# Selective scan on one core: two-step projections, remainders on TensorE, and two of twelve increments on GpSimd

## The chip, the cores and the metric

One core of a Trainium2 chip runs the whole program. The metric is device time in microseconds from start to end of one execution, lower is better. The engines are PE (TensorE: matmul, with PEld its weight load), DVE (VectorE), ACT (ScalarE), POOL (GpSimd) and SP (SyncE), which here issues all DMAs of the part that changes. A name with a q (SPq, PEq) is an engine's sequencer.

## The reference, cut to what matters

The program is a convolution-like state-space block, then an attention and an expert block; only the first is touched. `x` is 4 images of 192 channels and 32 x 32 positions, so L = 1024. After a group norm:

```python
# 4 directions k: row order, column order, and both reversed
xs    = stack([x0, x1, reversed(x0), reversed(x1)])
x_dbl = einsum('bkdl,kcd->bkcl', xs, x_proj_weight)       # 6 + 16 + 16 rows
dts, Bs, Cs = split(x_dbl)                                # 6, 16, 16
dt = softplus(einsum('bkrl,kdr->bkdl', dts, dt_projs_weight) + bias)
def step(h, ...):                  # 16 states for each of 192 channels
    h = h * exp(dt * A) + (dt * u) * B
    return h, sum over n of h * C
y = merge of the 4 directions of (scan(step) + Ds * u)
```

The states are 4 images x 4 directions x 192 channels x 16 = 49,152 recurrences of 1024 steps each.

## The kernel before, in words

`prepare` norms x into `s.X` (96 partitions, two halves of channels, 1024 positions) and readies the weights. `scan` then runs `Fori` over the 4 images with 8 **units** written out inside, 32 units in all. A unit is one direction (p: row or column order; r: forward or backward) and one half f of the channels, so 96 channels with 16 states each. It is cut into 12 **tiles** t of 8 channels x 16 states = 128 partitions x 1024 positions. A tile's scan runs in two halves (24 half tiles q, two for each t), as PSUM holds 512 columns to a bank. `n` counts units, `g` half tiles.

For each tile:

- SP loads `decay[:, t % 4, :]` with a broadcasting DMA (L632, `load`): 8 rows of dt, each repeated on 16 partitions, 128 x 4 KB = 512 KB. It is issued when tile t - 4 has been scanned (DR = 4 buffers).
- ACT makes exp(dt * A) of it in place (L501).
- PE spreads dt*u from `stack` over the 128 partitions (L425, a bf16 matmul with three bf16 parts stacked on 96 rows, so that nothing is lost) into a ring of 4 PSUM banks `psU`.
- DVE multiplies that by B (L558, `product`, one half tile ahead) and scans (L614); the second half starts from the last state of the first and waits for its end.
- POOL multiplies the states by C (L528), in place in `hs` (HR = 6 buffers).
- PE sums the 16 states of each channel, three tiles at a time (L387, `sum_states`, four trips a unit), into `psY`; DVE takes `psY` into `s.Y` after every second unit (L567 in row order, with the skip term D*u; L571 in column order, which reads and writes with a stride).

Between the tiles the next units' inputs are made. The projection of dt (L352 `project`, weights `w_dt` that `prepare` has multiplied out to 96 x 96 blocks) runs at half tiles 16 to 19 for the unit two ahead; ACT does softplus at t = 9 to 11 (L454 to L460), POOL adds its two terms at t = 9 (L538) and multiplies by u at t = 11 (L544), giving `dt` and `dtu`. SP stores `dt` to DRAM (`store`), from which the loads read. `dtu` is split into three bf16 parts by ACT (L468, L471) and POOL (L531, L534) at t = 2 to 6 of the next unit, and SP copies the parts to `stack` with 9 DMAs of 64 KB at t = 4, 5 and 7. B and C for a unit are projected by PE straight into their spread form of 128 rows and copied by ACT to `bc` (L480). ACT makes a turned copy `xt` of x for the column order (L510).

All engines run their instructions in the order written, and so does SP. The waits that set the order around a tile are these, in PE's and DVE's parts:

```python
pe.wait_ge(scan_done, g + (S0 - UR + 1))      # half tile q - 4 scanned: its bank is free
if q % 6 == 0: v.wait_ge(summed, ...)         # the hs buffer is free
v.wait_ge(decay_ready, n * TILES + (t + 1))   # exp made
```

## Time and profile before

| | us |
|---|---|
| time, median of 3 runs (lowest, highest) | 3095.22 (3094.96, 3102.87) |
| profiled execution, its own time | 3110.97 |
| its span | 3108.9 |
| first product of the scan to the last scan's start | 75.5 to 1540.3 |
| one unit of the scan, mean of 32 | 45.8 |
| mean granted clock of TensorE, as a share of 2.4 GHz | 0.834 |

The profile comes from the one profiled execution. "Busy" is the time in which an engine works on instructions; the idle time in brackets stands before an instruction, with what ended it. The granted clock is that which TensorE got: 1.00 stands for 2.4 GHz and 0.50 for 1.2 GHz. The DMA share is the mean busy share of the core's 16 DMA engines.

### The profile page before, as it was taken

Reading aid. Unit: us, or ns where it says so; the run is one execution under the profiler, and the core shown is the slowest. Engines: PE = TensorE matmul, PEld = TensorE weight load, DVE = VectorE, ACT = ScalarE, POOL = GpSimd, SP = SyncE. Lnnn points to the kernel's source line nnn. Section 1 sums busy time; section 2 is a strip of 40 time slices with the busy share of each in tenths; the row PEclk is TensorE's granted clock in tenths of the full one; section 3 lists DMA queues with packets and bytes.
Section 4 is the critical chain, followed back from the end, with each engine's and each line's share of the span. In section 5 each row is a group of like instructions: output and inputs, shape, how many; then the busy total and the mean of one; then the engine's idle time right before and its main releaser. Section 6 shows DMA issues by size and latency. Waiting matters only on the chain. (4 is left out here: it accounts for less than half of the span.)

```text
span 3108.9 us, 33979 instructions
## 1 busy us (share of the span) xinstructions
PE 2521.1 (81%) x9156; PEld 920.0 (30%) x9156; DVE 2223.0 (72%) x3030; ACT 1424.7 (46%) x1949; POOL 1311.6 (42%) x677
## 2 busy tenths in 40 slices
PE   4677677776677766776668689999999889999999
PEld 2111111111111111111124123232232246666766
DVE  4999999999999998999755688787878631111112
ACT  3444544445444444444456147676767522222221
POOL 1788878787788877788751100000000200000000
PEclk9777767777677777777758689999999889999999
DMA  3555555555555555555512603131313400000000
GB/s 88 144 167 165 160 152 166 154 155 159 157 168 162 166 146 152 160 152 163 152 47 80 104 2 43 23 42 24 42 23 42 87 1 6 5 5 5 5 5 10
DMA packets 101755, 286.76 MB, mean 92 GB/s; under 512 B 14878, under 2 KB 19137, under 8 KB 101569
## 3 DMA queue, kind: packets, MB, share of 16 engines
q1 hardware_dynamic: 100506, 284.94, 35.1%
q8 instruction: 52, 0.85, 0.1%
q14 instruction: 95, 0.78, 0.1%
q10 hardware_dynamic: 1102, 0.19, 0.0%
HBM read 239.66 MB, written 25.88 MB: 85 GB/s over the span
## 5 line engine op out<-in xcount | busy, mean ns | idle before, releaser
L528 POOL TENSOR_TENSOR hs<-hs,bc 128x1024 f32<-128x1024 f32 x384 | 900.4, 2355 | 224.9 <-DVE hs L614 224.2
L501 ACT ACTIVATE decay<-decay,a_neg 128x1024 f32<-128x1024 f32 x384 | 440.4, 1148 | 666.2 <-DMA decay<-dt_rows 652.3
L425 PE MATMUL psU<-stack,spread_sel 96*128 96x512 bf16 x768 | 361.1, 487 | 425.0 <-DVE hs L614 346.3
L1446 DVE TENSOR_REDUCE mx<-ps 128x1 f32<-128x512 f32 x864 | 539.3, 682 | 117.7 <-PE ps L1285 112.4
L558 DVE TENSOR_TENSOR psU<-psU,bc 128x512 f32<-128x512 f32 x768 | 514.4, 673 | 25.9 <-issue 13.4
L1421 ACT ACTIVATE P<-ps 128x512 f32<-128x512 f32 x768 | 417.6, 599 | 249.3 <-PE ps L1297 225.2
L614 DVE TENSOR_TENSOR_SCAN hs<-decay,psU 128x512 f32<-128x512 f32 x384 | 464.7, 1210 | 72.6 <-PE psY L387 52.4
L614 DVE TENSOR_TENSOR_SCAN hs<-decay,hs,psU 128x512 f32<-128x512 f32 x384 | 487.5, 1269 | 1.1
L387 PE MATMUL psY<-hs,state_sel 128*32 128x512 f32 x1572 | 401.5, 855 | 23.2 <-DVE Y L571 11.2
L1719 DVE SCALAR_TENSOR_TENSOR acc<-psE,gate,acc 128x192 f32<-128x192 f32 x128 | 53.4, 417 | 448.5 <-PE psE L1619 445.5
L1285 PE MATMUL ps<-ks,qs 96*128 96x512 bf16 x864 | 345.0, 404 | 34.8 <-DMA ks<-qk_parts 24.2
L425 PEld LDWEIGHTS psU<-stack,spread_sel 96*128 96x128 bf16 x768 | 71.1, 100 | 992.2 <-DVE hs L614 818.4
L1610 PE MATMUL psH<-Zf,w 96*128 x768 | 334.3, 592 | 1.1 <-DVE pr L1677 1.1
L1657 ACT ACTIVATE hid<-psH,b 128x512 f32<-128x512 f32 x192 | 131.5, 687 | 382.5 <-PE psH L1610 382.5
L1297 PE MATMUL ps<-qs,ks 99*128 99x512 bf16 x768 | 294.4, 383 | 0.0
L1619 PEld LDWEIGHTS psE<-w,hid 128*128 128x128 f32 x1536 | 251.2, 190 | 13.4 <-issue 13.4
L1619 PE MATMUL psE<-w,hid 128*128 128x192 f32 x1536 | 254.2, 326 | 0.0
L1310 PE MATMUL psO<-P,v_now 128*32 128x512 f32 x1536 | 206.2, 609 | 0.0
L1610 PEld LDWEIGHTS psH<-Zf,w 96*128 96x128 f32 x768 | 144.7, 190 | 171.8 <-issue 170.8
L1285 PEld LDWEIGHTS ps<-ks,qs 96*128 96x128 bf16 x864 | 83.8, 98 | 314.7 <-DVE mx L1446 233.1
L1225 POOL COPY v_now<-V 128x1024 f32 (+1 forms) x15 | 15.5, 1038 | 320.1 <-PE psO L1310 320.0
L1217 POOL TENSOR_TENSOR nm<-zero,top 128x32 f32<-128x32 f32 x13 | 3.3, 253 | 344.5 <-DVE top L1450 344.5
(237 smaller groups left out, 2280.3 us busy)
## 6 DMA issues: line engine op xcount, KB each, us to landing
decay<-dt_rows SPq DMA_DIRECT2D x388, 512.0 KB
stack<-parts SPq DMA_DIRECT2D x297, 64.0 KB, 5.5
dt_rows<-dt SPq DMA_DIRECT2D x33, 384.0 KB, 7.1
qs<-qk_parts SPq DMA_DIRECT2D x90, 128.0 KB, 6.7
ks<-qk_parts SPq DMA_DIRECT2D x90, 128.0 KB, 7.2
qk_parts<-qparts SPq DMA_DIRECT2D x16, 576.0 KB, 3.7
w<-in_L_ffn_w_dram SPq DMA_DIRECT2D x8, 576.0 KB, 9.9
X<-in_x_dram SPq DMA_DIRECT2D x4, 768.0 KB, 9.7
```

What stands on the lines that cost most here:

```text
L387: m = pe.matmul(psY[BLK * j:BLK * j + BLK, c, :], s.state_sel[:, trip, :], hs[:, (3 * trip + j) % HR, CH * c:CH * c + CH], start=(trip == ...
L425: pe.matmul(psU[:, q % UR, :], s.spread_sel[:, gg, :], stack[:, ui % 2, j, CH * pos:CH * pos + CH], start=True, stop=True).then_inc(dtu_sp ...
L501: nc.scalar.activation(decay[:, t % DR, :], decay[:, t % DR, :], ACT.Exp, scale=s.a_neg[:, col:col + 1]).then_inc(decay_ready, 1)
L528: pool.tensor_tensor(h, h, bc[:, 2 * p + r, 1, :], ALU.mult).then_inc(hc_ready, 1)
L558: v.tensor_tensor(u, u, bc[:, 2 * p + r, 0, CH * pos:CH * pos + CH], ALU.mult).then_inc(dbu_ready, 1)
L614: v.tensor_tensor_scan(h, da, du, init, ALU.mult, ALU.add).then_inc(scan_done, 1)
L1285: m = pe.matmul(ps1[:, bank, :], qs[0:KQ, hg, head, 128 * qt:128 * qt + 128], ks[0:KQ, hg, head, CH * c:CH * c + CH], start=True, stop=not ...
L1297: m = pe.matmul(ps2[:, bank, :], ks[0:KM, hg, head, 128 * kt:128 * kt + 128], qs[0:KM, hg, head, CH * qc:CH * qc + CH], start=True, stop=n ...
L1421: nc.scalar.activation(P[:, kt % 2, head, :], ps2[:, bank, :], ACT.Exp).then_inc(exp_done, 1)
L1446: v.reduce_max(mx[:, slot, u:u + 1], ps1[:, (slot * MAXES + u) % R, :], AX.X).then_inc(max_done, 1)
L1610: m = pe.matmul(psH[:, t % 3, :], w1[:, e, f, 128 * t:128 * t + 128], s.Z[:, b, f, CH * c:CH * c + CH], start=(f == 0), stop=(f == 1))
L1619: m = pe.matmul(psE[:, tt % 2, 0:D], hid[:, e % 2, t, 128 * tt:128 * tt + 128], w2[:, e, t, :], start=(t == 0), stop=(t == HT - 1))
```

## The change: what it does

Prepared weights: `w_dt` is no longer multiplied out. A projection now runs in two steps: `inputs` (two matmuls with `w_xd`, 128 rows that hold the 6 + 32 rows of both r of one p) gives `xd` once for each image and p, and `steps` makes the 96 rows of a unit from 6 rows of it. B and C of `xd` go to DRAM (`keep_xd`) and come back spread over 128 partitions by DMA (`load_bc`, two DMAs of 512 KB for each of the four directions of an image, at t = 2 and 4 of units 5, 6, 7 and 0).

The order of units becomes f, p, r, so all four directions add up in `psY` and ACT takes it after four units (`take`); PE adds the skip term itself (`skip`, with a diagonal). There is no `xt`: PE and POOL read and write in column order with a stride (`turned`, and `h.rearrange` in `sum_states`).

The second and third bf16 part of dt*u come from TensorE (`remainder`: identity times `dtu` minus the parts known, in `psP`, which ACT casts), so POOL's two subtractions go.

For tiles 5 and 11 (POOL_TILES) there is no spread by PE and no product by DVE. SP loads the 8 rows of dt*u from DRAM (`keep_dtu`, `load_rep`, 512 KB each), POOL multiplies them by B, and ACT writes its exp for these tiles into `psU`.

The making of dt and dt*u moves forward: softplus from t = 9 to 11 to t = 5 to 7, the sum and the product on POOL from t = 9, 11 to t = 4, 5, the first cast from t = 4 of the next unit to t = 11. `hs` gets 8 buffers and `decay` 6.

The diff, cut to its core:

```diff
-        HR, DR, UR = 6, 4, 4
+        HR, DR, UR = 8, 6, 4
+        POOL_TILES = (5, 11)
 # TensorE
+                def inputs(out, nb, p, c):
+                    for h in range(2):
+                        m = pe.matmul(out, s.w_xd[:, p, h, :], turned(s.X[:, nb, h, :], p)[:, 16 * c:16 * c + 16, :],
+                                      start=(h == 0), stop=(h == 1))
+                    m.then_inc(xd_proj, 1)
+                def remainder(c, known, ready):
+                    cs = slice(CH * c, CH * c + CH)
+                    m = pe.matmul(psP[0:HC, c, :], s.ident[0:HC, 0:HC], dtu[:, cs], start=True, stop=False)
+                    for i in range(known):
+                        m = pe.matmul(psP[0:HC, c, :], s.minus_bf[:], parts[:, i, cs], start=False, stop=(i == known - 1))
+                    m.then_inc(ready, 1)
...
-                                pe.wait_ge(scan_done, g + (S0 - UR + 1))
-                                pe.matmul(psU[:, q % UR, :], s.spread_sel[:, gg, :],
-                                          stack[:, ui % 2, j, CH * pos:CH * pos + CH],
-                                          start=True, stop=True).then_inc(dtu_spread, 1)
-                                z_side(q, *unit_ahead(b, ui), n + 2)
-                                bc_side(q, b, ui, n)
+                                if t not in POOL_TILES:
+                                    pe.wait_ge(scan_done, g + (S0 - UR + 1))
+                                    pe.matmul(psU[:, q % UR, :], s.spread_sel[:, gg, :],
+                                              stack[:, ui % 2, j, CH * pos:CH * pos + CH],
+                                              start=True, stop=True).then_inc(dtu_spread, 1)
+                                if t == 1:
+                                    pe.wait_ge(mid_ready, n * 2 + (c + 3))
+                                    remainder(c, 2, tail_ready)
+                                if t == 3:
+                                    if c == 0:
+                                        pe.wait_ge(xd_ready, nb * 4 + (2 * order(nu)[1] + 2))
+                                    pe.wait_ge(lo_ready, n * 2 + (c + 3))
+                                    steps(nu, c)
+                                if t == 6 and ui in XD_UNITS:
+                                    pe.wait_ge(z_taken, n * 2 + 6)
+                                    inputs(psP[:, c, :], (b + 1) % NB, XD_UNITS[ui], c)
+                                if t == 10:
+                                    if c == 0:
...
+                                        pe.wait_ge(dtu_ready, n + 3)
+                                        pe.wait_ge(hi_ready, n + 3)
+                                    remainder(c, 1, rest_ready)
 # ScalarE
+                            to = at = decay[:, t % DR, :]
+                            if t in POOL_TILES:
+                                to = psU[:, 2 * t % UR:2 * t % UR + 2, :]
...
+                                act.wait_ge(scan_done, n * (2 * TILES) + (2 * t - 2 + S0))
...
+                            if t == 11:
+                                act.wait_ge(stacked[(ui + 1) % 2], in_stack(b, ui + 1))
+                                act.wait_ge(dtu_ready, n + 3)
+                                nc.scalar.copy(parts[:, 0, :], dtu[:]).then_inc(hi_ready, 1)
 # GpSimd
+                            if t + 3 in POOL_TILES:
+                                i = POOL_TILES.index(t + 3)
+                                pool.wait_ge(rep_landed[i], n * 16 + 16)
+                                pool.tensor_tensor(rep[:, i, :], rep[:, i, :], bc[:, slot, 0, :], ALU.mult).then_inc(rep_ready, 1)
 # SyncE
+                def load_dt(slot, t):
+                    d = rows_of(t)
+                    src = s.dt_dram[slot, d:d + DD, :].unsqueeze(1).broadcast_to([DD, N, L])
+                    sp.dma_start(decay[:, t % DR, :], src).then_inc(landed[t % DR], 16)
+                def load_rep(slot, i):
+                    src = s.dtu_dram[slot, i].unsqueeze(1).broadcast_to([DD, N, L])
+                    sp.dma_start(rep[:, i, :], src).then_inc(rep_landed[i], 16)
+                def load_bc(slot, which=(0, 1)):
+                    p, r = slot // 2, slot % 2
+                    for i in which:
+                        at = BLK * r + N * i
+                        src = s.bc_dram[p, at:at + N, :].unsqueeze(0).broadcast_to([DD, N, L])
+                        sp.dma_start(bc[:, slot, i, :], src).then_inc(bc_landed[slot], 16)
...
+                load_bc(0)
+                sp.wait_ge(dt_ready, 1)
+                keep_dt(0)
...
+                for t in range(DR):
+                    load_dt(0, t)
+                sp.wait_ge(dtu_stored, 32)
+                for i in range(2):
+                    load_rep(0, i)
+                for part, (ready, n) in enumerate(((hi_ready, 1), (mid_ready, 2), (lo_ready, 2))):
+                    sp.wait_ge(ready, n)
+                    stack_up(part, 0)
+                load_bc(1)
+                load_bc(2)
...
+                            if t == 2 and ui in (5, 6, 7, 0):
+                                sp.wait_ge(hc_ready, n * TILES + (TILES + START))
+                                load_bc((ui - 5) % UNITS, (0,))
+                            if t == 4 and ui in (5, 6, 7, 0):
+                                load_bc((ui - 5) % UNITS, (1,))
...
+                            if t in POOL_TILES:
...
+                                load_rep((ui + 1) % 4, i)
```

At the end of `scan` SP waits for every load that was issued, those for a unit that doesn't come among them, as it did before.

## Rows read from the trace of the kernel before

**Rows 1.** The page: busy time of each engine, and DMA share in tenths

```profile
PE 2521.1 (81%) x9156; PEld 920.0 (30%) x9156; DVE 2223.0 (72%) x3030; ACT 1424.7 (46%) x1949; POOL 1311.6 (42%) x677
...
DMA  3555555555555555555512603131313400000000
```

**Rows 2.** Busy time by window: the scan, from first product to last scan

```profile
core 0: us, PE busy (x) PEld busy (x) DVE busy (x) ACT busy (x) POOL busy (x), PEclk, DMA share, GB/s
75.50:1541.00 1465.50, 1034.24 (x2827) 228.33 (x2827) 1373.96 (x1552) 684.45 (x709) 1171.21 (x509) 0.73 0.54 158
```

**Rows 3.** Who waited for whom in 130 to 1500 us: total, times, longest

```profile
ACT decay L501 <- DMA decay<-dt_rows: 609.0, 299, 5.1
...
DVE hs L614 <- PE psY L387: 49.3, 43, 2.0
...
DVE hs L614 <- ACT decay L501: 18.2, 24, 1.6
```

**Rows 4.** DMA issues in 130 to 1500 us

```profile
decay<-dt_rows SPq DMA_DIRECT2D x360, 512.0 KB
```

**Rows 5.** Two windows of 2 us in the scan (columns as in rows 2)

```profile
514.00:516.00 2.00, 2.00 (x4) 0.53 (x2) 2.00 (x3) 0.00 (x0) 1.79 (x2) 0.50 0.51 125
...
540.00:542.00 2.00, 1.80 (x9) 0.25 (x7) 2.00 (x3) 0.67 (x2) 2.00 (x2) 1.00 0.51 203
```

**Rows 6.** Two units that follow each other (columns as in rows 2)

```profile
683.30:736.10 52.80, 32.78 (x92) 7.68 (x95) 45.49 (x52) 22.32 (x24) 39.14 (x18) 0.69 0.55 153
736.10:778.70 42.60, 30.03 (x87) 6.44 (x81) 40.24 (x46) 24.16 (x24) 34.00 (x16) 0.74 0.53 158
```

**Rows 7.** DVE in order of time: start, length, instruction

```profile
501.50 1.21 DVE L614 TENSOR_TENSOR_SCAN hs<-decay,psU 128x512 f32<-128x512 f32 x1
502.63 0.68 DVE L558 TENSOR_TENSOR psU<-psU,bc 128x512 f32<-128x512 f32 x1
503.21 1.27 DVE L614 TENSOR_TENSOR_SCAN hs<-decay,hs,psU 128x512 f32<-128x512 f32 x1
...
504.98 1.21 DVE L614 TENSOR_TENSOR_SCAN hs<-decay,psU 128x512 f32<-128x512 f32 x1
```

**Rows 8.** Groups by line and shape, 0 to 1850 us

```profile
L528 POOL TENSOR_TENSOR hs<-hs,bc 128x1024 f32<-128x1024 f32 x384 | 900.4, 2355 | 224.9 <-DVE hs L614 224.2
...
L501 ACT ACTIVATE decay<-decay,a_neg 128x1024 f32<-128x1024 f32 x384 | 440.4, 1148 | 666.2 <-DMA decay<-dt_rows 652.3 <-issue 13.3
...
L531 POOL TENSOR_TENSOR rest<-dtu,parts 96x1024 f32<-96x1024 f32 x32 | 68.0, 2125 | 14.4 <-ACT parts L468 14.3
...
L468 ACT CAST parts<-dtu 96x1024 bf16<-96x1024 f32 x33 | 34.0, 1030 | 2.5 <-DVE dtu L580 2.5
...
L571 DVE TENSOR_TENSOR Y<-Y,psY 96x1024 f32 x8 | 16.0, 2006 | 0.0
...
L567 DVE SCALAR_TENSOR_TENSOR Y<-X,d_sum,psY 96x1024 f32 x8 | 10.0, 1251 | 0.0
```

**Rows 9.** PE in order of time, at 1.2 GHz (first two) and 2.4 GHz

```profile
503.31 1.93 PE L387 MATMUL psY<-hs,state_sel 128*32 128x512 f32 x6
...
578.52 1.91 PE L352 MATMUL psP<-xt,w_c 96*128 96x512 f32 x2
...
585.80 1.02 PE L352 MATMUL psP<-xt,w_c 96*128 96x512 f32 x2
```

**Rows 10.** All engines in order of time: start of the scan

```profile
21.94 5.43 PE L206 MATMUL ps_prep<-wdt,wx 6*96 6x192 f32 x16 [1.10 <-DVE wdt L233]
...
51.09 2.67 SPq L632 DMA_DIRECT2D decay<-dt_rows  x4
...
74.88 0.61 PE L425 MATMUL psU<-stack,spread_sel 96*128 96x512 bf16 x1 [11.71 <-DMA stack<-parts]
```

**Rows 11.** All engines in order of time: after the scan

```profile
1549.94 1.91 DVE L571 TENSOR_TENSOR Y<-Y,psY 96x1024 f32<-96x1024 f32 x1 [8.37 <-PE psY L387]
...
1552.14 2.09 SPq L801 DMA_DIRECT2D raw<-in_x_dram  x4
```

More of the change, by code:

```diff
@@ L266, in _ @@
                 own.wait()
+                v.wait_ge(gp, 3)
+                for f in range(2):
+                    own(v.tensor_scalar(s.d_diag[:, f, :], s.ident[0:HC, 0:HC], s.d_sum[:, f:f + 1], None, ALU.mult))
+                own(v.tensor_scalar(s.minus_bf[:], s.ident[0:HC, 0:HC], -1.0, None, ALU.mult))
+                own.wait()
+        nc.clear_and_free_semaphores(sems)
+        nc.all_engine_barrier()
 def scan(nc, w, s):
@@ L380, in sum_states, with steps @@
-                def sum_states(n, pair, r, trip, c, first=None):
+                def inputs(out, nb, p, c):
[3 more added lines that the diff above has]
+                    m.then_inc(xd_proj, 1)
+                def steps(nu, c):
+                    f, p, r, k = order(nu)
+                    pe.matmul(psP[0:HC, c, :], s.w_dt[BLK * r:BLK * r + R, p, HC * f:HC * f + HC],
+                              xd[BLK * r:BLK * r + R, p, CH * c:CH * c + CH], start=True, stop=True).then_inc(z_proj, 1)
@@ new lines, in remainder, with skip @@
+                def remainder(c, known, ready):
[4 more added lines that the diff above has]
+                    m.then_inc(ready, 1)
+                def skip(b, f, c):
+                    pe.matmul(psY[0:HC, c, :], s.d_diag[:, f, :], s.X[:, b, f, CH * c:CH * c + CH], start=True, stop=False)
@@ L382, in sum_states @@
+                def sum_states(n, ui, trip, c):
+                    p = order(ui)[1]
                     if c == 0:
-                        if trip == 0 and r == 0:
-                            pe.wait_ge(y_taken, pair + (1 + START))
                         pe.wait_ge(hc_ready, n * TILES + (TILES + 3 * trip + 3 + START))
                     for j in range(NBLK):
+                        h = hs[:, (ui * TILES + 3 * trip + j) % HR, :]
+                        h = h.rearrange("p (w h) -> p h w", h=HH) if p else h.rearrange("p (h w) -> p h w", h=HH)
@@ new lines, in z_end, with part @@
+                def z_end(n1):
+                    act.wait_ge(z_taken, n1 * 2 + 2)
+                    nc.scalar.activation(soft[:], soft[:], ACT.Exp, scale=-1.0).then_inc(exp_own, 1)
+                    act.wait_ge(exp_own, n1 + 1)
+                    nc.scalar.activation(soft[:], soft[:], ACT.Ln, bias=s.one[0:HC, :]).then_inc(log_ready, 1)
+                def part(i, n1, c, rest, ready):
+                    act.wait_ge(rest, n1 * 2 + (c + 1))
+                    nc.scalar.copy(parts[:, i, CH * c:CH * c + CH], psP[0:HC, c, :]).then_inc(ready, 1)
@@ new lines, in take @@
+                def take(b, f, last):
+                    act.wait_ge(summed, last + SUM0)
+                    nc.scalar.copy(s.Y[:, b, f, :], psY[0:HC, :, :].rearrange("p c l -> p (c l)")).then_inc(y_taken, 1)
+                nc.scalar.preload_act_table_set("natural_log_exp_and_others")
+                for p in range(2):
+                    for c in range(2):
+                        act.wait_ge(xd_proj, 2 * p + c + 1)
+                        nc.scalar.copy(xd[:, p, CH * c:CH * c + CH], (psU if p else psP)[:, c, :]).then_inc(xd_ready, 1)
@@ new lines, in _ @@
+                for c in range(2):
+                    z_half(0, 0, c)
+                z_end(0)
+                act.wait_ge(dtu_ready, 1)
+                nc.scalar.copy(parts[:, 0, :], dtu[:]).then_inc(hi_ready, 1)
+                for c in range(2):
+                    part(1, 0, c, rest_ready, mid_ready)
+                for c in range(2):
+                    part(2, 0, c, tail_ready, lo_ready)
+                act.wait_ge(dt_stored, 16)
+                for c in range(2):
+                    z_half(1, 1, c)
@@ L494, in _ @@
+                z_end(1)
+                act.wait_ge(stacked[0], STACK_INC)
+                act.wait_ge(dtu_ready, 2)
+                nc.scalar.copy(parts[:, 0, :], dtu[:]).then_inc(hi_ready, 1)
                 with act.Fori(0, NB, 1) as b:
@@ L506, in _ @@
[L506 to L512 removed]
+                            if t == 1:
+                                for c in range(2):
+                                    part(1, n + 1, c, rest_ready, mid_ready)
@@ new lines, in _ @@
+                            if t == 3:
+                                for c in range(2):
+                                    part(2, n + 1, c, tail_ready, lo_ready)
+                            if t == 4 and ui % 4 == 0:
+                                take(b if ui else (b + (NB - 1)) % NB, 1 - f, n * SUB)
+                            if t == 5:
+                                act.wait_ge(dtu_ready, n + 2)
+                                act.wait_ge(dt_stored, n * 16 + 32)
+                                z_half(nu, n + 2, 0)
```

420 lines of the change are left out of this document (193 added, 227 removed).

## The prediction

> **What bounds the kernel now.** I read the page first [rows 1]: DVE looks like the engine to relieve, and the DMA engines look half idle, at five tenths in every slice of the scan. The window over the scan alone [rows 2] puts numbers on both: DVE busy 1374 of 1465.5 us (94%), POOL 80%, PE 71% at a granted clock of 0.73, DMA share 0.54. A unit is 1465.5 / 32 = 45.8 us.
>
> Then DVE in order of time [rows 7]. From 501.50 to 504.98 is one tile with no gap: scan 1.13, product 0.58, scan 1.19, product 0.58 (start to start), 3.48 us. Twelve tiles are 41.8 us, and the takes (8 of 1.25 and 8 of 2.01 us in 32 units [rows 8]) add 0.8. With some 0.2 at the end of a unit that makes 42.8, so DVE stands still for 3.0 us of a unit. The waits [rows 3] say for whom: sums of PE (49 us in 30 units) and exps of ACT (18). Neither is a busy engine. ACT itself waits 609 us, and for one thing: the decay loads.
>
> The DMA share is the row that the reader is to look at twice. A share of 0.50 that never falls can be 16 engines half idle or 8 of them never idle. Two windows decide it [rows 5]: both show 0.51, while one moves 125 GB/s and the other 203. If the engines had slack, the share would go up and down with the bytes. It stays at one half while the speed changes by 1.6, so eight engines are always busy, and what varies is how long a packet takes. Two neighbouring units show what that does [rows 6]: the same work takes 52.8 us at 153 GB/s and 42.6 us at 158, with the share 0.55 and 0.53; DVE works 45.5 and 40.2 us of them (the windows cut tiles, so these differ a little), that is 86% and 94%. The short unit is DVE's own 42.8, the long one is not.
>
> So two things stand within a few per cent of each other: DVE (42.8 us a unit) and the eight DMA engines that carry the decay loads. Their account, from rows 2: of the 0.54, 0.50 are these eight, always on. The other 0.04 x 16 engines over 8 engines is 8% of 45.8 = 3.7 us a unit in which the upper eight work too; that is the stack copies and the store of dt, which use all 16 and so cost the lower eight the same 3.7. There remain 42.1 us for 12 loads [rows 4]: **3.51 us a load** of 512 KB as a mean. The windows give its bounds, 524 KB at 203 GB/s = 2.6 us and at 125 = 4.2.
>
> **The change, part by part.**
>
> *DVE.* Each of the two POOL tiles loses two products of 0.58; one of the scans now has to wait for the full end of the one before (1.21 after its start, not 1.13, plus the signal), which gives 0.1 back. 2 x 1.05 = 2.1 us a unit. The takes go to ACT: 0.8. DVE comes to 42.8 - 2.9 = 39.9 us.
>
> *POOL.* Minus two subtractions of 2.1 [rows 8], plus two products of 2.35 less overlap: 12 + 2 + 2 operations of 2.31 = 37.0 us, as before. With a stride, which no POOL row here has, dt*u costs between 2.35 and 1.6 times that (DVE with and without: 2.01 and 1.25 [rows 8]); I take 1.6 in half the units, mean 37.7. It hides under 39.9.
>
> *PE.* A float32 matmul of 512 columns is a pair of 1.91 us at the low clock and 1.02 at the high one [rows 9]. Out go 8 pairs of projections and 4 bf16 spreads; in come 4 pairs and 6 bf16 (remainders), 2 pairs (steps), 1 (inputs), 0.5 (skip). That is equal within a pair. Reading `hs` with a stride in half the units is unknown: from nothing to 1.6 times, which would lift 4 trips x 2 x 1.93 = 15.4 us by 9 at worst. PE now: 1034/32 = 32.3; then up to 37 as a mean. Hidden; I take nothing.
>
> *ACT* is at 21 us a unit and stays there: two casts of 1.03 become one and four halves, one take in four units is added.
>
> *A new wait.* PE's remainder at t = 10 stands between the spreads of half tiles 20 and 21 and waits for `hi_ready` n + 3. ACT makes it after the exp of tile 11, which may not write `psU` until tile 9 is scanned. So from the end of tile 9: exp 1.05, cast 1.03, remainder 0.5 + 0.2 to 1.0 + 0.4 behind a signal each (0.1), spread 0.4 to 0.6: product 21 comes 3.7 to 4.9 us later, and DVE has nothing else, as scan 20 stands behind product 21. I take 4.0: DVE's unit is **43.9**, and the shortening that DVE was to get is nearly gone. ACT's exp of tile 5 has the same wait for tile 3, but DVE has 3.0 us of tile 4 to do in that time and the exp takes 1.15, so it is free.
>
> *SP and the DMAs.* Nothing is taken from the queue: still 12 decay loads (also for tiles 5 and 11), 9 copies, one store. Added for each unit: 2 loads of dt*u (512 KB each), one of B or C (8 for 8 units), two small stores of 8 rows (one packet an engine, 3.51/16 = 0.22 us each) and a quarter of an `xd` store. The dt*u load has the form of the decay load. The B and C load repeats 16 rows 8 times, its outer size is 8 too, but no row of before shows it: at best it uses 16 engines (half of 3.51), at worst it is a decay load. I take a decay load, the nearest row.
>
> The unit's DMA time is then 15 x 3.51 + 3.7 + 0.5 = **56.9 us** on the same eight engines, against 43.9 for DVE, 38 for POOL and 37 for PE. Its bounds are 15 x 2.6 + 4.2 = 43.2 and 15 x 4.2 + 4.2 = 67. Deeper buffers (6, 8) do not help: they cover lateness, not a lack of throughput.
>
> On that load the Trainium skill (DMA: Bandwidth & Descriptors, section on why a DMA increments its semaphore by 16) says that a DMA is spread over the largest number up to 16 that divides the outermost sizes of both sides, always the lowest-numbered ones. By it every load here gets 8, as the share of 0.50 in rows 5 agrees with, and B and C too; were those on 16, the unit would be 55.1.
>
> *Start and end.* Before, PE's 5.4 us of multiplied-out weights delayed the norm (DVE waited 5.9) [rows 10]; that goes, the scan begins some 4 us earlier. But before the first spread the queue must now move 2 B/C, 6 decay and 2 dt*u loads, and then the 9 copies, not 4 and 9. The queue starts at about 44 rather than 51; 44 + 10 x 3.51 + 3.7 + 3 for the store's round trip = 86 against 74.9 [rows 10]. From there 4 + 32 x 15 = 484 loads and 32 x 4.2 are to be moved, and SP waits for all: 86 + 1699 + 134 = 1919. Before, the same count, 74.9 + 384 x 3.51 + 32 x 3.7 = 1541, is the scan's end [rows 2], and the block ended at 1552 [rows 11] with the last sums, under which its last loads lay; now the loads end last. 1919 - 1552 = 367 us more. What follows the scan is the same.
>
> **The sum.** The profiled execution spans 3108.9 and took 3110.97; the same with the change would be 3476. It lies 15.8 us (0.5%) over the median of the runs, 3095.2, so the median goes to 3095 + 367 = 3462, I say **3460 us**, 12% slower.
>
> **Rivals.**
>
> *A, the one forecast (0.69):* bound by eight DMA engines at 3.0 to 3.8 us a load, 3210 to 3600 by the same count. For it: the constant 0.51 and the unit of 52.8 us that the same work took when packets were slow.
>
> *B, the same bound with faster packets (0.11):* 2.8 to 3.0 us. The copies come in one bunch a unit instead of three, so the stream is disturbed less often. At 3.0 us the count is 80 + 484 x 3.0 + 134 = 1666, 114 more, 3209; at 2.8 it is 78 + 1355 + 134 = 1567, 3110.
>
> *C, faster (0.13):* the loads take 2.6 us throughout, as in the second window of rows 5, because the long packets of before come from something that the change removes. Then 43.2 us of DMA lie under 43.9 of DVE and its new wait: 32 x (43.9 - 45.8) = -61, start +2 to +5, so about 3040. It decides from 2.7 us a load downward, where the count falls under 1552. Against it: within the trace of before 3.51 is the mean of 388 loads, and at the very start, with no other engine at work, the queue was no faster: four loads and nine copies from 51.1 to 74.9 [rows 10]. The skill's page on DMA gives a limit of some 358 GB/s for a core's HBM traffic (section Specifications); the new unit moves 8.9 MB, which by that would take 25 us and bound nothing; no window of the scan comes near it.
>
> *D, slower still (0.04):* column order. If PE reads a stride of 32 floats at a fourth of its speed, the sums of those units cost 15.4 x 3 = 46 us more, PE comes to 78 us in half the units, the mean is (78 + 57)/2 = 67.5, and the time 3095 + 367 + 32 x 10.6 = 3800. The skill (SBUF — State Buffer, the note on cachelines in its section on ports) speaks for some price of such strides. DVE's 2.01 against 1.25 [rows 8] says 1.6, with which D does not happen.
>
> *E, no change (0.03):* a load of 2.7 to 2.8 us, where the count gives the 1552 of before.
>
> **How the numbers follow.** The forecast is A's time at the mean of before. The range holds A and B whole, 3110 (2.8 us a load) to 3600 (3.8 us): 0.69 + 0.11 = 0.80; C, D and E lie outside. It is that wide because one number, the time of a load, carries all of it, and the trace has it anywhere between 2.6 and 4.2 us. About 0.3% (9 us) is what a measurement of this kernel cannot tell from no change. Faster is C, 0.13; the same is E, 0.03; slower is A, B and D, 0.84.
>
> **What would show it.** Right: in the scan the DMA share stays at 0.55 or so with DVE's busy share down to 70%; GB/s hardly above 160 as a mean; ACT waits for decay, dt*u or both, and now DVE waits for ACT's exp in most tiles; units of some 57 us; the scan's DMAs outlast its last scan. Wrong: a share below 0.5 in parts of each unit, or GB/s near 200 all through, units of 44 us, and a gap of 4 us on DVE before half tile 21. The prediction fails most easily on 3.51 us, which I measured but cannot derive.

## The result, and the profile after

| | before | after |
|---|---|---|
| time, median (lowest, highest; runs) | 3099.05 (3094.96, 3114.12; 4) | 3321.32 (3314.73, 3326.98; 4) |
| ratio to before, 95% interval | | 1.0707 [1.0662, 1.0752] |
| span of the profiled execution | 3108.9 | 3325.1 |
| mean granted clock of TensorE | 0.834 | 0.828 |

The medians here and below are of all runs; the ratios leave out a run that took over 1.5% longer than the fastest of its kernel. The change makes the kernel 222 us slower. The prediction said 3460 us with a range of 3110 to 3600: slower, as forecast, by about 60% of the size.

The page of the kernel after: busy time, the DMA share in tenths, and GB/s in the same 40 slices. The rows of before are [rows 1].

```profile
PE 2608.1 (78%) x9176; PEld 912.0 (27%) x9176; DVE 2125.1 (64%) x2885; ACT 1418.1 (43%) x1994; POOL 1342.0 (40%) x675
...
DMA  4555555555555555555553170322223130000000
GB/s 100 161 162 169 157 177 194 160 178 175 154 194 189 166 160 172 196 167 171 187 165 113 58 115 2 40 27 35 35 27 40 21 81 5 5 5 5 5 5 10
```

DVE has lost 98 us of work while the span has grown by 216, so the time went into waiting. The DMA row still reads five tenths throughout, but the bytes a second went up: 173 GB/s in the scan against 158 [rows 2]. The window over the scan, from first product to last scan:

```profile
core 0: us, PE busy (x) PEld busy (x) DVE busy (x) ACT busy (x) POOL busy (x), PEclk, DMA share, GB/s
109.10:1761.40 1652.30, 1127.26 (x2857) 227.03 (x2859) 1282.96 (x1408) 676.03 (x754) 1206.63 (x511) 0.73 0.53 173
```

A unit is now 51.6 us (1652.3 / 32) against 45.8. DVE works 40.1 us of it against 42.9 and stands still for 11.5 against 2.9. The 216 us of the span by stretch:

| stretch | before | after | change |
|---|---|---|---|
| start to first product | 75.5 | 109.1 | +33.6 |
| first product to last scan's start | 1464.8 | 1652.3 | +187.5 |
| last scan's start to the next part's first load | 11.8 | 12.7 | +0.9 |
| everything behind | 1556.8 | 1551.0 | -5.8 |

The next view is of the waits in 130 to 1500 us (total, times, longest), and it names what DVE waits for. Compare [rows 3]: there ACT's wait for the loads was 609 us, here it is 291 and, for the exps that go to `psU`, 33.

```profile
ACT psU L528 <- DVE hs L645: 342.6, 44, 12.2
DVE psU L602 <- PE psU L431: 298.7, 92, 8.6
ACT decay L528 <- DMA decay<-dt_rows: 290.9, 153, 7.1
...
PE psP L369 <- ACT parts L553: 164.4, 27, 10.0
...
DVE hs L645 <- ACT decay L528: 5.3, 6, 2.2
```

DVE waits 299 us for PE's spread and 5 us for ACT's exp. If the loads set the pace, most of the wait would be for exps, since that is how a load of dt reaches DVE. (There is a second way, which these rows hide; it comes below.) Where in the unit DVE waits is found by adding up the idle times in DVE's order of time by half tile, over 32 units: before product 21 it is 196 us (6.1 a unit, in all 32 of them, never under 5.0), before 13 or 14 it is 70 us, nearly all of it in units 4 and 6 of each image (counted from 0), and before 8 it is 54. Before the first product of a unit it is only 14, in the first unit of the last three images (4.5 to 4.7 each); the remaining 35 us are scattered. One of the 32 places before product 21, by DVE, ACT and PE in order of time:

```profile
1031.63 1.27 DVE L645 TENSOR_TENSOR_SCAN hs<-decay,hs,psU 128x512 f32<-128x512 f32 x1
1038.05 0.70 DVE L602 TENSOR_TENSOR psU<-psU,bc 128x512 f32<-128x512 f32 x1 [5.15 <-PE psU L431]
...
1032.94 1.12 ACT L528 ACTIVATE psU<-decay,a_neg 128x1024 f32<-128x1024 f32 x1 [3.58 <-DVE hs L645]
1033.99 1.03 ACT L553 CAST parts<-dtu 96x1024 bf16<-96x1024 f32 x1
...
1029.82 0.57 PE L431 MATMUL psU<-stack,spread_sel 96*128 96x512 bf16 x1
1035.16 1.99 PE L369 MATMUL psP<-dtu,ident 96*96 96x512 f32 x2 [4.77 <-ACT parts L553]
1036.95 0.63 PE L371 MATMUL psP<-parts,minus_bf 96*96 96x512 bf16 x1
1037.38 0.63 PE L431 MATMUL psU<-stack,spread_sel 96*128 96x512 bf16 x1
```

The reader is to follow the chain from top to bottom: the second scan of tile 9 ends at 1032.90; ACT's exp of tile 11, which had waited for it, ends at 1034.06; the cast ends at 1035.02; PE's remainder pair and its bf16 part end at 1037.6; the spread at 1038.0; and only then DVE has a product to make. These are 5.15 us, in which DVE has nothing. PE had no work for 4.77 us before its remainder, which then ran at 1.2 GHz: 1.99 us is the low clock's time [rows 9].

In 21 of the 32 places the gap is that of these rows, or within 0.3 us of it. In the other 11 it is 6.3 to 8.7 us, because the exp of tile 11 waited longer, not for the scan but for its own load. This is the second way from the loads to DVE: by the exp, the cast, the remainder and the spread, so it stands in the row of DVE's waits for PE. What goes beyond the usual 5.15 us comes to 31 us in all. One of the 11:

```profile
411.27 1.12 ACT L528 ACTIVATE psU<-decay,a_neg 128x1024 f32<-128x1024 f32 x1 [4.01 <-DMA decay<-dt_rows]
...
416.39 0.70 DVE L602 TENSOR_TENSOR psU<-psU,bc 128x512 f32<-128x512 f32 x1 [8.65 <-PE psU L431]
```

### The profile page after: what moved, and what is told of

The parts are those of the page before. It is cut to its first block and busy times, and to the rows that moved or that the text cites. A ratio compares the mean times of both kernels' runs of the same rounds, so it can differ in the third digit from the quotient of the medians.

```text
span 3325.1 us, 34486 instructions
## 1 busy us (share of the span) xinstructions
PE 2608.1 (78%) x9176; PEld 912.0 (27%) x9176; DVE 2125.1 (64%) x2885; ACT 1418.1 (43%) x1994; POOL 1342.0 (40%) x675
## 5 line engine op out<-in xcount | busy, mean ns | idle before, releaser
L602 DVE TENSOR_TENSOR psU<-psU,bc 128x512 f32<-128x512 f32 x640 | 431.3, 678 | 394.1 <-PE psU L431 393.6
L385 PE MATMUL psY<-hs,state_sel 128*32 128x512 f32 x1560 | 502.5, 1054 | 41.4 <-POOL hs L571 35.9
L528 ACT ACTIVATE decay<-decay,a_neg 128x1024 f32<-128x1024 f32 x320 | 364.7, 1149 | 330.0 <-DMA decay<-dt_rows 329.5
L431 PE MATMUL psU<-stack,spread_sel 96*128 96x512 bf16 x640 | 284.0, 470 | 256.7 <-DVE hs L645 256.2
L645 DVE TENSOR_TENSOR_SCAN hs<-decay,hs,psU 128x512 f32<-128x512 f32 x320 | 406.8, 1271 | 2.3
L645 DVE TENSOR_TENSOR_SCAN hs<-decay,psU 128x512 f32<-128x512 f32 x320 | 386.6, 1208 | 8.0 <-ACT decay L528 8.0
L369 PE MATMUL psP<-dtu,ident 96*96 96x512 f32 x268 | 200.5, 841 | 242.2 <-ACT parts L553 196.6
L431 PEld LDWEIGHTS psU<-stack,spread_sel 96*128 96x128 bf16 x640 | 60.1, 102 | 828.7 <-DVE hs L645 597.2
L528 ACT ACTIVATE psU<-decay,a_neg 128x1024 f32<-128x1024 f32 x64 | 71.5, 1118 | 454.4 <-DVE hs L645 413.8
```

Source lines behind the costliest of these rows:

```text
L385: m = pe.matmul(psY[BLK * j:BLK * j + BLK, c, :], s.state_sel[:, trip, :], h[:, 16 * c:16 * c + 16, :], start=False, stop=(trip == SUB - 1 ...
L431: pe.matmul(psU[:, q % UR, :], s.spread_sel[:, gg, :], stack[:, ui % 2, j, CH * pos:CH * pos + CH], start=True, stop=True).then_inc(dtu_sp ...
L528: nc.scalar.activation(to, at, ACT.Exp, scale=s.a_neg[:, col:col + 1]).then_inc(decay_ready, 1)
L602: v.tensor_tensor(u, u, bc[:, 2 * p + r, 0, CH * pos:CH * pos + CH], ALU.mult).then_inc(dbu_ready, 1)
L645: v.tensor_tensor_scan(h, da, du, init, ALU.mult, ALU.add).then_inc(scan_done, 1)
```

## The experiments

The ratio is always to the kernel before on the same chip, in the same job. "Scan" runs in this table, and in the windows of the experiments, from the start of the first scan (3 to 6 us behind the first product) to the start of the last, and a unit is a 32nd of it. By this measure a unit is 45.6 us before the change and 51.5 after it.

| kernel | median us | ratio, 95% interval | scan, us | share, GB/s |
|---|---|---|---|---|
| before | 3099.05 | | 79.8 to 1540.3 | 0.54, 159 |
| after | 3321.32 | 1.0707 [1.0662, 1.0752] | 112.2 to 1761.4 | 0.53, 174 |
| before_plus3 | 3163.08 | 1.0195 [1.0121, 1.0269] | 78.4 to 1601.2 | 0.55, 185 |
| before_plus6 | 3316.34 | 1.0613 [1.0529, 1.0697] | 78.1 to 1744.5 | 0.54, 199 |
| before16 | 3077.43 | 0.9909 [0.9882, 0.9936] | 73.8 to 1513.9 | 0.65, 170 |
| after16 | 3294.67 | 1.0618 [1.0559, 1.0677] | 98.0 to 1730.2 | 0.79, 185 |
| after_late | 3203.89 | 1.034 [1.026, 1.0419] | 107.5 to 1635.1 | 0.55, 188 |
| after16_late | 3196.93 | 1.0279 [1.0244, 1.0314] | 92.9 to 1625.5 | 0.83, 197 |
| mix | 3213.63 | 1.0291 [1.0211, 1.0371] | 105.1 to 1660.1 | 0.55, 184 |
| mix16 | 3097.21 | 0.9976 [0.9951, 1.0002] | 91.9 to 1534.9 | 0.88, 209 |
| after_cast | 3170.59 | 1.0203 [1.0148, 1.0257] | 113.5 to 1604.9 | 0.55, 192 |
| after16_cast | 3188.3 | 1.0285 [1.0234, 1.0336] | 97.9 to 1607.5 | 0.85, 199 |
| mix16b | 3101.37 | 0.9988 [0.9965, 1.0012] | 78.4 to 1537.3 | 0.87, 208 |

In the expectations, D is the theory of the prediction (the eight DMA engines bound the changed kernel) and W its rival (the new waits in the order of the engines do).

**1. before_plus3: is the kernel before at the limit of the eight DMA engines?** Three loads of the decay load's form are added to each unit. They read 8 rows of the input into a buffer that nobody reads; the rest is unchanged.

```diff
+                            if t in (1, 5, 9):
+                                sp.wait_ge(spare_in, n * 48 + (16 * (t // 4) + 16))
+                                sp.dma_start(spare[:], w.x[0, 0:DD].rearrange("d h w -> d (h w)").unsqueeze(1)
+                                             .broadcast_to([DD, N, L])).then_inc(spare_in, 16)
```

> The kernel before with three more loads of 512 KB in each unit, in the form of the decay load (8 rows of x, repeated 16 times), into a spare buffer that nobody reads; no engine waits for them. Theory D: a unit grows by three loads, 3 x 3.15 to 3 x 3.51 = 9.5 to 10.5 us less the slack of 0.5, so 3095 + 32 x 5.8 to 10 = 3280 to 3415; 3280 is what the changed kernel's own loads of 3.15 us give. Rival W: within 15 us of 3095.

Measured: 1.0195 [1.0121, 1.0269], 3163 us. A quarter more loads lengthens the unit from 45.6 to 47.6 us, so a load more costs 0.65 us, not 3.5. Neither expectation held: 3163 lies between D's 3280 and W's 3095. The share stays at 0.55 and the GB/s rise from 158 to 185. The eight engines that looked never idle had a good part of their speed left.

**2. before_plus6: and where does it end?** The same with six extra loads a unit (at every odd t), again into a buffer that nobody reads.

> The kernel before with six more loads of 512 KB a unit (one at each odd t) into the spare buffer. Three more cost 1.8 us a unit. If a load really takes the 3.51 us that the trace of before gives, 18 loads are 67 us, time 3770. If the engines keep 2.5 to 2.9 us a load when they always have work, 18 loads and 3.7 are 49 to 56 us, time 3200 to 3420.

Measured: 1.0613 [1.0529, 1.0697], 3316 us. The next three loads cost 4.5 us a unit (52.1 against 47.6), so this kernel is near a limit for much of the time, though not for all. By the prediction's account it spends (52.1 - 3.7) / 18 = 2.7 us a load. Window and waits of before_plus6:

```profile
core 0: us, PE busy (x) PEld busy (x) DVE busy (x) ACT busy (x) POOL busy (x), PEclk, DMA share, GB/s
78.10:1744.50 1666.40, 1016.94 (x2814) 222.17 (x2812) 1383.63 (x1549) 684.70 (x709) 1168.93 (x508) 0.71 0.54 199
```

```profile
PE psU L427 <- DMA stack<-parts: 187.6, 25, 9.9
...
DVE hs L616 <- ACT decay L503: 131.9, 87, 5.2
```

```profile
SPq L661 <- DMA spare<-in_x_dram: 711.5, 157, 9.8
```

This is what a kernel looks like whose loads come late throughout: 199 GB/s, PE waits for the stack copies behind them, and DVE waits 132 us for exps. The share is 0.54, as in the kernel before that moves 158 GB/s. The share does not tell the two apart; the waits do. Part of the lateness is the experiment's own: there is one spare buffer, so SP, which issues in order, waited 711 us in 130 to 1500 us for the spare load before to land, and every decay load behind it waited too (before_plus3 has no such row). So 2.7 us is an upper value for what a load costs on these engines.

**3. before16 and after16: the same loads on sixteen engines.** `dt` (and dt*u) is stored twice in DRAM, so that the outer size of a load is 16; the bytes of a load are the same.

```diff
-                src = s.dt_dram[par, d:d + DD, :].unsqueeze(1).broadcast_to([DD, N, L])
+                src = s.dt_dram[par, d:d + DD, :, :].rearrange("d c l -> (d c) l").unsqueeze(1).broadcast_to([2 * DD, N // 2, L])
```

> The kernel before, with dt kept twice in DRAM so that a decay load has 16 source rows, each repeated 8 times, in place of 8 rows repeated 16 times: the same bytes into the same places, an outermost size of 16. Theory D (eight DMA engines bound both kernels): the loads spread over 16 engines, the DMA share varies with the bytes, DVE's stalls of 3.0 us a unit go, unit 42.8 to 43.5, time 3010 (2995 to 3035). Rival W (DMA was never a bound, what costs is the order of waits on PE, ACT and DVE): 3095, unchanged.

> The changed kernel with dt and dt*u kept twice in DRAM, so that decay and dt*u loads have 16 source rows (B and C loads as they are). Theory D: the DMA bound goes, what is left is DVE's 39.9 and its wait of 5 us at half tile 21: unit 46 (shortest unit now), time 3321 - 32 x 5.5 - 12 at the start = 3130 (3090 to 3180). Rival W (the 12.3 us that DVE stands before products are all the order of waits): within 30 us of 3321.

Measured: before16 0.9909 [0.9882, 0.9936], after16 1.0618 [1.0559, 1.0677]. The share rises to 0.65 and 0.79, so the loads do use more engines. The rule of the Trainium skill that the prediction weighed (DMA: Bandwidth & Descriptors, the section on why a DMA increments its semaphore by 16), by which the outer sizes set the count, agrees with these shares. Window and waits of after16:

```profile
98.00:1730.20 1632.20, 1114.20 (x2849) 225.12 (x2846) 1278.18 (x1407) 667.13 (x754) 1207.36 (x511) 0.74 0.79 185
```

```profile
DVE psU L602 <- PE psU L431: 289.7, 73, 10.8
...
ACT decay L528 <- DMA decay<-dt_rows: 92.8, 49, 4.0
```

ACT's wait for the loads falls from 291 to 93 us (for the exps that go to `psU`, which have a scan to wait for as well, it goes from 33 to 88), and the wait of DVE for PE hardly moves, from 299 to 290. The time falls by 27 us out of 222 (3294.67 against 3321.32), 14 of which lie ahead of the first scan (98.0 against 112.2). D, which asked for 3130, falls here: loads on sixteen engines do not set the changed kernel free. They are not quite out of it, though. The gap before product 21 is 209 us in after16, no less than the 196 of the changed kernel, and in 12 of its 32 places the exp of tile 11 still waits for its load (45 us beyond the usual 5.15). All 12 are in units 5, 7 and 0 of an image, where SP also issues loads of B and C, which this run left on 8 rows.

before16 is the fastest kernel of the study, some 28 us (0.9% of 3110) below before; here too neither expectation held (3010, or no change). Its schedule is unchanged, DVE's wait for exps (18 us before) is gone, and ACT's for loads falls from 609 to 435.

**4. after_cast: one line.** ACT makes the first cast one tile earlier, ahead of the exp of tile 11, which has to wait for tile 9. All work is done, and the loads are unchanged.

```diff
-                            if t == 11:
+                            if t == 10:
                                 act.wait_ge(stacked[(ui + 1) % 2], in_stack(b, ui + 1))
                                 act.wait_ge(dtu_ready, n + 3)
                                 nc.scalar.copy(parts[:, 0, :], dtu[:]).then_inc(hi_ready, 1)
```

> The changed kernel with one thing moved on ACT: the first cast of the next dt*u stands before the exp of tile 11 (at t = 10) and no longer behind it, so PE's remainder at t = 10 need not wait for the end of tile 9. Nothing on PE, DVE, POOL or in the loads is changed. Theory W: the 6.1 us a unit before product 21 fall to about 1 (PE's own 2.6 us of remainder stay between two spreads), worth up to 160 us. Theory D says that with 8 source rows the DMA engines (15 x 2.7 to 3.0 + 4.2 = 45 to 49) take over: 3200 to 3260, and then some of the wait comes back as waits for spreads or exps.

Measured: 1.0203 [1.0148, 1.0257], 3171 us, 151 less than after. Window, waits, and the same place of a unit in order of time:

```profile
113.50:1604.90 1491.40, 1065.01 (x2852) 218.28 (x2846) 1280.51 (x1407) 673.35 (x754) 1202.72 (x510) 0.77 0.55 192
```

```profile
DVE psU L602 <- PE psU L431: 149.2, 76, 7.6
...
PE psP L369 <- ACT parts L553: 10.7, 6, 2.7
```

```profile
1037.05 1.03 ACT L553 CAST parts<-dtu 96x1024 bf16<-96x1024 f32 x1
1038.22 1.07 PE L369 MATMUL psP<-dtu,ident 96*96 96x512 f32 x2 [1.16 <-ACT parts L553]
1039.12 0.38 PE L371 MATMUL psP<-parts,minus_bf 96*96 96x512 bf16 x1
1039.15 1.12 ACT L528 ACTIVATE psU<-decay,a_neg 128x1024 f32<-128x1024 f32 x1 [1.08 <-DVE hs L645]
1039.34 0.38 PE L431 MATMUL psU<-stack,spread_sel 96*128 96x512 bf16 x1
1039.76 0.70 DVE L602 TENSOR_TENSOR psU<-psU,bc 128x512 f32<-128x512 f32 x1 [0.64 <-PE psU L431]
```

The cast now runs beside the scans of tile 9 instead of behind them, PE waits 1.16 us instead of 4.77 and is still at the high clock (1.07 for the pair, 0.38 for the spread), and DVE's gap is 0.64. Before product 21 DVE's idle time falls from 196 to 8 us over 32 units, 188 less; 28 us each come up before product 3 (for PE) and before scan 22 (for POOL's product). The scan is 158 us shorter. With the loads untouched, the unit comes to 46.6 us, which is (46.6 - 4.2) / 15 = 2.8 us a load by the prediction's account. The loads speed up as soon as they are asked to.

**5. after_late and after16_late: the other way to take the wait out.** The first remainder moves from t = 10 to t = 0 of the next unit, with eight and with sixteen engines; the pair of remainders that stood ahead of the first unit goes with it.

```diff
-                                if t == 10:
+                                if t == 0:
                                     if c == 0:
...
                                     remainder(c, 1, rest_ready)
```

> The changed kernel with the first remainder of the next unit moved on PE from t = 10 to t = 0 of the next unit, behind the spread, so that no spread waits for the exp of tile 11. Loads as in the changed kernel. Theory D: DVE's wait moves elsewhere (to exps or to the spreads), the time stays within 60 us below 3321, since 15 loads of 3.15 us and 4.2 are 51.4 us a unit. Rival W: the whole 12.3 us a unit goes, 2930; half of it, 3125.

> The changed kernel with the first remainder at t = 0 of the next unit and with 16 source rows. Theory D: with the wait before product 21 gone the DMA engines are the next bound of the run with 8 source rows (unit 47.7), so this one falls by 60 us or more below its 3204. Theory W: within 25 us of 3204, as its stalls stand at the unit's start behind remainders.

Measured: 1.034 [1.026, 1.0419] and 1.0279 [1.0244, 1.0314]. The unit is 47.7 us, and the gap of 6.1 is gone. The time of 3204 is neither D's (3261 or more) nor W's (2930, or 3125 for half): what DVE still waits lies before products 1, 2, 8, 13 and 14 and before scan 22 (27 to 45 us each), and part of it is new, behind the moved remainders. Sixteen engines give 7 us here (3204 against 3197), which is less than the runs of after_late differ among themselves (3191 to 3229).

**6. mix and mix16: PE's work spread out.** Remainders at t = 1 and 2, `steps` at t = 4, `inputs` at t = 8.

```diff
-                                if t == 1:
+                                if t == 2:
                                     pe.wait_ge(mid_ready, n * 2 + (c + 3))
                                     remainder(c, 2, tail_ready)
-                                if t == 3:
+                                if t == 4:
...
                                     steps(nu, c)
```

> The changed kernel with every piece of side work on PE put where no spread stands close behind it: first remainder of the next unit at t = 1 (was t = 10 of the unit before), second at t = 2 (was 1), steps at t = 4 (was 3, beside sums), inputs at t = 8 (was 6); ACT's casts and SP's copies follow. Theory W (what the change costs is the order of waits on PE: 6.1 us a unit before product 21, 1.7 before product 8, 2.2 before products 13 and 14, 2.7 at the unit's start): some 10 of these 12.7 us go, unit 42, time 3020. Theory D, in the form that the last runs leave (the eight DMA engines can do a load in 2.6 to 2.9 us when kept full): 15 loads and 4.2 us are 43 to 48, so the unit stays at 45 to 47 and the time at 3110 to 3170.

> The same with dt and dt*u kept twice in DRAM, so that 14 of 15 loads have 16 source rows. Theory D: it gains 60 to 150 us over the run without (3000 to 3050). Theory W: within 25 us of it.

Measured: mix 1.0291 [1.0211, 1.0371], mix16 0.9976 [0.9951, 1.0002]. Here sixteen engines are worth some 100 us by the ratios (116 by the medians). Both of mix's expectations missed: its 3214 lies above W's 3020 and above D's 3110 to 3170; and mix16 gained what D said, but came to 3097 and not to 3000 to 3050. Window of mix16, and what PE waited for in mix:

```profile
91.90:1534.90 1443.00, 1038.21 (x2852) 212.90 (x2846) 1282.47 (x1407) 671.64 (x758) 1200.91 (x510) 0.77 0.88 209
```

```profile
PE psP L369 <- ACT parts L480: 106.2, 25, 7.4
```

So the loads are second in line: apart from the 31 us before product 21 they do not set the changed kernel's time, but they do set mix's, or share in it. The new order did not take the waits out, it moved them: in mix DVE waits 80 us before product 5, behind the second remainder, which waits for ACT's casts, which stand behind exps; and 67 us before scan 22, for ACT's exp and POOL's product of tile 11. In mix16 the first falls to 34, the second stays at 64. mix varied by 66 us between its four runs (3170 to 3236), and its profile is the slowest of them, so its unit of 48.6 us is an upper value.

**7. after16_cast: both at once.**

> The same with 16 source rows. Without the cast moved, 16 rows gave 27 us. If both bounds were at work together, moving the cast gives more here: 3110 to 3160, 130 to 180 below the 3295 of the changed kernel with 16 rows.

Measured: 1.0285 [1.0234, 1.0336], 3188 us. This missed: with sixteen engines it is no faster than after_cast with eight (18 us slower by the medians, but the two intervals overlap). The units are nearly the same (47.2 against 46.6 us), DVE's idle time before product 3 and scan 22 has grown to 44 and 49 us over 32 units, from 28 each. Why mix gains from sixteen engines and this order does not stays open.

**8. mix16b: an earlier start, and POOL one tile earlier.** Three decay loads and the nine copies go ahead of the other loads in the queue, and POOL multiplies the loaded dt*u four tiles ahead rather than three.

```diff
-                for t in range(DR):
+                for t in range(3):
                     load_dt(0, t)
-                sp.wait_ge(dtu_stored, 32)
-                for i in range(2):
-                    load_rep(0, i)
...
-                            if t + 3 in POOL_TILES:
+                            if t + 4 in POOL_TILES:
```

> The run with all side work on PE put elsewhere and 16 source rows, plus two things: at the start the 9 copies go out after 3 decay loads (not behind 6 and 2 of dt*u), and POOL makes the product of a POOL tile 4 tiles ahead, not 3 (DVE waited 2.0 us a unit before half tile 22). Start 5 to 10 us earlier, 1 to 2 us a unit: 3030 to 3070, which would be 1 to 2% under the kernel before.

Measured: 0.9988 [0.9965, 1.0012], 3101 us. This missed too. The first scan comes 13.5 us earlier (78.4 against 91.9), but the last scan does not (1537.3 against 1534.9). Most of the gain is gone within the first unit, which takes 62.0 us against 46.0 in mix16:

```profile
108.16 0.68 ACT L469 ACTIVATE dt<-psP,cols 96x512 f32<-96x512 f32 x1 [14.31 <-DMA dt_rows<-dt]
110.54 1.15 ACT L523 ACTIVATE decay<-decay,a_neg 128x1024 f32<-128x1024 f32 x1 [1.12 <-DMA decay<-dt_rows]
...
111.72 1.22 DVE L640 TENSOR_TENSOR_SCAN hs<-decay,psU 128x512 f32<-128x512 f32 x1 [11.80 <-ACT decay L523]
```

ACT may not write dt anew until the store of dt has landed. In mix16 the same ACT instruction starts at 107.67, so the scan reaches this place earlier in mix16b but the queue does not: ACT stands 14 us for the store, and DVE 12 us for the exp behind it. The two changes of this run were not made one at a time, so what POOL's earlier product is worth isn't known; DVE's wait before scan 22 fell from 64 to 34 us.

## Why the prediction was right in sign and off in size

It forecast A, bound by the eight DMA engines, and A's time by its own account fits what was measured: (51.6 - 4.2) / 15 is 3.16 us a load, inside A's 3.0 to 3.8. That is a coincidence, and so the forecast was right by luck: after16 and after_cast show that the time is set by something else in the main.

**The step that failed: that 3.51 us a load stays.** It was read as what a load costs on engines that are never idle, from a share of 0.50 whatever the GB/s [rows 5]. before_plus3 and before_plus6 show that it is not a cost but what is left over: at 12 loads a unit one takes 3.5 us, at 18 it takes 2.7, with the same share. The share reports that the engines hold packets, not that they could not move more. The prediction's DMA time was 56.9 us a unit; at 2.7 us it is 15 x 2.7 + 4.2 = 44.7, level with the prediction's 43.9 for DVE and well under the measured 51.6. The prediction saw 2.6 us in a window, and made of it rival C and a bound, when it was the row to go by.

**DVE's unit, 39.9 us:** measured 40.1 of work.

**The new wait, 4.0 us (3.7 to 4.9):** the right place, the right chain, the wrong size: never under 5.0 and 6.1 in the mean. Two terms were off. The remainder was priced at 0.5 to 1.0 us, which is half of a pair; it is a whole one, 1.02 to 1.99. And PE has stood idle for 4 to 10 us before it and is then at the low clock: in 31 of the 32 places the pair took 1.99 us. So the upper value is the rule: 1.12 + 1.03 + 1.99 + 0.63 + 0.63, less overlap, is the 5.15 of the rows. What lies above that, 1 us in the mean, comes from an exp that was itself late, because its load was. At 196 us this is the largest piece of the loss; taking it away gave 151 us.

**PE, "hidden, I take nothing":** its sum was right (35.2 us a unit against "up to 37"), and yet this was the second error. PE has time enough, but not between two spreads. Ahead of the spread for product 8 stand `steps` and half a trip of sums, 2.0 and 1.9 to 2.2 us at the low clock. Ahead of those for 13 and 14 stand, in units 4 and 6 of an image, `inputs` (also `skip` in unit 4) and sums. Products 8 and 13 or 14 cost 54 + 70 us. In order, DVE's unit is 40.1 + 6.1 + 1.7 + 2.2 + 0.4 at its start + 1.1 elsewhere = 51.6, as measured. (The expectation of mix put 2.7 at the unit's start; that was wrong.) The loads come into it with some 39 us: the 31 in the gap before product 21, and 8 that DVE waited directly for exps.

**The strides:** POOL's dt*u took 2.87 us in column order and 2.38 in row order, 1.2 times and not 1.6; POOL's unit is the 37.7 us of the prediction all the same (1206.6 / 32). PE's sums with a stride are another matter. Half a trip (x6 in the rows) took 2.22 to 2.25 us in all 128 column-order cases, whatever the clock; in row order it took 1.93 at the low clock and 1.06 at the high one. So the stride costs 1.15 times at 1.2 GHz and 2.1 times at 2.4, where the prediction had nothing to 1.6. Rival D, a quarter of the speed, is gone. These are the rows; in the window over the first of the sums the granted clock is 1.00:

```profile
399.80 2.87 POOL L584 TENSOR_TENSOR dtu<-dt,X 96x1024 f32<-96x1024 f32 x1
450.04 2.38 POOL L584 TENSOR_TENSOR dtu<-dt,X 96x1024 f32<-96x1024 f32 x1
```

```profile
119.10 2.22 PE L385 MATMUL psY<-hs,state_sel 128*32 128x512 f32 x6
...
402.29 1.93 PE L385 MATMUL psY<-hs,state_sel 128*32 128x512 f32 x6
...
624.56 1.06 PE L385 MATMUL psY<-hs,state_sel 128*32 128x512 f32 x6
```

```profile
119.10:121.32 2.22, 2.22 (x8) 0.22 (x7) 2.22 (x4) 0.00 (x0) 1.78 (x1) 1.00 0.52 127
```

**The start, 86 us:** it is 109.1, and 33.6 of the 222 us. The order of the start shows why:

```profile
60.55 3.77 SPq L665 DMA_DIRECT2D decay<-dt_rows  x6
64.36 6.07 SPq L669 DMA_DIRECT2D rep<-dtu_rows  x2
70.47 10.43 SPq L680 DMA_DIRECT2D stack<-parts  x9
...
99.54 1.04 ACT L512 CAST parts<-dtu 96x1024 bf16<-96x1024 f32 x1 [29.11 <-DMA stack<-parts]
100.69 1.99 PE L369 MATMUL psP<-dtu,ident 96*96 96x512 f32 x2 [34.17 <-ACT parts L512]
...
109.14 0.70 DVE L602 TENSOR_TENSOR psU<-psU,bc 128x512 f32<-128x512 f32 x1 [36.20 <-PE psU L431]
```

The first decay load is issued at 60.55, where I had the queue start at 44, because the two-step projection has dt of the first unit ready later (its store is issued at 54.65, against 48.08 before). Then the queue takes from 60.6 to 99.5 to bring eight loads and nine copies. And ACT may cast unit 1 only when the nine copies have landed (29 us of idle), and PE makes two remainders of unit 1 from it, and twelve matmuls into `psY` that used to lie in the wait, before its first spread: 8.0 us from 100.69 to 108.71 that the prediction did not count. The place in the queue of the stack copies, behind eight loads, was seen. In mix16b, with the copies ahead and on sixteen engines, the first product is made at 75.3.

**The end, "the loads end last, 1919":** it is 0.9 us longer than before. The loads do end last, but by a few us only: ACT's last take ends at 1770.5, and the next part starts at 1774.1.

## What to carry to other kernels

A share of DMA engines that stays level says how many engines hold packets, not that they are at their limit; before pricing added transfers at the mean duration of the old ones, ask what would show a limit (waits that reach the bounding engine), and, where one can, add a few dead transfers, each with a buffer of its own so that the queue never waits for them, and read the slope. Work that is put between two steps that feed the bounding engine is priced by the gap it opens there, not by the sum of the engine: walk the order of one whole unit, with every wait that stands ahead of such a step. If the time fits the forecast, that still does not show its cause: here two kernels were needed, one that takes the supposed bound away and one that takes its rival away.

## What the runs showed of the hardware

- The time of a 512 KB load from 8 rows went from 3.51 us at 12 loads a unit to 2.7 at 18, at a share of 0.54 to 0.55 in both, and 158 against 199 GB/s. Other engines do not explain it: in the start of the changed kernel the DMAs ran at 131 to 154 GB/s with hardly another engine at work, and right behind the scan, with PE at work, at 206 to 209. What sets which of the two speeds comes stays open; nothing was run on it.

```profile
76.00:84.00 8.00, 0.00 (x0) 0.00 (x0) 0.00 (x0) 0.00 (x0) 0.00 (x0) 0.50 0.63 143
84.00:92.00 8.00, 0.00 (x0) 0.00 (x0) 0.00 (x0) 0.00 (x0) 0.00 (x0) 0.50 0.52 131
...
1762.00:1766.00 4.00, 2.27 (x9) 0.15 (x6) 0.66 (x1) 0.00 (x0) 3.10 (x2) 1.00 0.52 209
1766.00:1770.00 4.00, 3.44 (x12) 0.30 (x6) 0.00 (x0) 0.51 (x1) 0.00 (x0) 1.00 0.51 206
```

- Sixteen engines do not double anything: the most that any kernel moved over its scan is 209 GB/s at a share of 0.88 (mix16), and with eight engines it was 199 at 0.54 (before_plus6). It is no fixed limit: the second unit below moved 244.
- Half a trip of PE's float32 sums, read from SBUF with a step of 32 elements, took 2.2 us both in windows with a granted clock of 1.00 and in windows with 0.50; without the step it took 1.06 and 1.93. These sums gained nothing from the high clock.
- Left open: why no kernel with the change beats before16. In mix16 DVE works 40.1 us of a unit of 45.1, so 5.0 us of waiting are left. They are not spread evenly. Units 2, 3 and 4 of an image take 41.4 to 41.6 us in the mean of the four images, under the 45.0 of before16; units 0, 1, 5, 6 and 7 take 45.4 to 50.8, and all but one of these are the units in which B and C are loaded, from 8 rows. Two units of mix16, number 4 and number 7 of the first image:

```profile
266.80:308.40 41.60, 32.17 (x100) 7.86 (x99) 40.01 (x46) 22.29 (x26) 37.81 (x17) 0.84 0.81 220
398.50:449.80 51.30, 35.39 (x92) 6.82 (x90) 40.47 (x45) 22.91 (x25) 40.35 (x18) 0.77 0.92 244
```

  Moving or shortening those loads was not tried, so that they are the cause is not shown.
